# P V of both tiles in one matmul in two attention stages, and a normalisation moved to ScalarE

## The reference

```
x = x + tanh(g_xattn[i]) * attention_i(layernorm(x), ctx)
x = x + tanh(g_ffn[i])   * ffn_i(layernorm(x))
```

```
scores = q k^T / sqrt(8)          # 64 x 64; attention 2: where(mask, scores, -1e9)
attn   = softmax(scores)          # attention 3: stablemax
out    = attn v                   # 64 x 8
x      = x + gate * (cat(out over heads) Wo + bo)
```

## Time and profile before

| | us |
|---|---|
| median of 3 runs (2514.01 to 2516.51) | 2514.34 |
| profiled execution | 2513.01 |
| its span in the profile | 2511.2 |
| TensorE busy | 2146.8 (85%) |
| VectorE busy | 1787.9 (71%) |
| ScalarE busy | 1350.6 (54%) |
| GpSimd busy | 1157.7 (46%) |

### The profile page before, as it was taken

How to read it: one execution, slowest core, us unless ns; L and a number is a source line. 1 busy time by engine, 2 the same in 40 slices (tenths; PEclk the granted TensorE clock), 3 DMA queues, 4 the chain that set the end, 5 groups by cost and what they waited for, 6 DMA issues and landing times. The chain is left out here.

```text
span 2511.2 us, 81208 instructions
## 1 busy us (share of the span) xinstructions
PE 2146.8 (85%) x33432; PEld 1717.8 (68%) x33443; DVE 1787.9 (71%) x5105; ACT 1350.6 (54%) x2499; POOL 1157.7 (46%) x1712
## 2 busy tenths in 40 slices
PE   6999999999995969999555799998399958898597
PEld 5887878787874746777444577776399947777375
DVE  3777777777773648887896589886555559988354
ACT  3555555555551327886998455553122259979232
POOL 1333333434343541113776125555466666876444
PEclk8999999999997979998677899997699979989699
DMA  6330000000005621110000111111487622332363
GB/s 194 110 123 27 25 27 25 24 21 20 20 18 152 180 85 55 55 58 17 1 1 3 32 37 52 52 51 36 134 235 230 185 75 79 106 96 79 101 185 103
DMA packets 225233, 195.14 MB, mean 78 GB/s; under 512 B 34444, under 2 KB 197846, under 8 KB 224864
## 3 DMA queue, kind: packets, MB, share of 16 engines
q1 hardware_dynamic: 186336, 143.52, 19.6%
q0 software_dynamic: 18944, 36.98, 4.2%
q10 hardware_dynamic: 19584, 9.44, 1.3%
HBM read 113.53 MB, written 70.55 MB: 73 GB/s over the span
## 5 line engine op out<-in xcount | busy, mean ns | idle before, releaser
L617 POOL DMA_INDIRECT slots<-row,put x256 | 258.1, 1008 | 211.5 <-issue 131.2
L1968 PE MATMUL experts_H<-experts_xs_t,experts_w 128*128 128x256 f32 (+1 forms) x832 | 253.5, 456 | 9.9 <-DMA experts_w<-in_F_w 4.7
L1102 ACT ACTIVATE l_prob_t<-l_banks 128x512 f32<-128x512 f32 x256 | 132.2, 603 | 145.9 <-PE l_banks L1219 115.4
L1968 PEld LDWEIGHTS experts_H<-experts_xs_t,experts_w 128*128 128x128 f32 x832 | 156.7, 195 | 74.5 <-issue 54.0
L1474 POOL TENSOR_TENSOR l_var_eps<-l_mv,eps 128x1 f32<-128x1 f32 x64 | 12.1, 189 | 413.9 <-DVE l_mv L1555 413.9
L1277 PE MATMUL l_banks<-l_val,l_prob_t 128*64 128x18 f32 x5120 | 201.1, 215 | 0.0
L1277 PEld LDWEIGHTS l_banks<-l_val,l_prob_t 128*64 128x64 f32 x5120 | 190.3, 143 | 8.1 <-issue 0.7
L1510 DVE TENSOR_REDUCE l_top<-l_S 128x16 f32<-128x1024 f32 x64 | 78.3, 1224 | 161.7 <-PE l_S L1653 161.7
L1986 PE MATMUL experts_Y<-experts_w,experts_hid 128*128 128x128 f32 x1600 | 190.0, 275 | 3.5 <-DVE experts_y L1912 2.6
L1986 PEld LDWEIGHTS experts_Y<-experts_w,experts_hid 128*128 128x128 f32 x1600 | 184.3, 192 | 5.0 <-issue 4.9
L1823 POOL DMA_INDIRECT rows<-experts_y,experts_idx x144 | 139.9, 971 | 90.0 <-DVE experts_y L1908 52.9
(11 more groups left out here) (312 smaller groups left out, 5943.4 us busy)
## 6 DMA issues: line engine op xcount, KB each, us to landing
experts_w<-in_F_w SPq DMA_DIRECT2D x136, 256.0 KB
l_ctx_t<-in_ctx_t SPq DMA_DIRECT2D x96, 128.0 KB, 2.4
early_q_m<-l_q_t SPq DMA_DIRECT2D x384, 32.0 KB, 1.8
experts_xs<-slots SPq DMA_DIRECT2D x72, 132.0 KB
experts_w<-in_F_w ACTq DMA_DIRECT2D x72, 128.0 KB, 3.3
slots<-l_empty SPq DMA_DIRECT2D x16, 536.0 KB, 4.1
experts_xs<-slots SPq DMA_DIRECT2D x16, 536.0 KB
slots<-l_empty SPq DMA_DIRECT2D x16, 520.0 KB, 5.9
```

The lines of the kernel that those rows point to most:

```text
L617: pool.indirect_dma_start(self.slots, bass.IndirectOffsetOnAxis(ap=g.put[c][:, tile:tile + 1], axis=0), g.row[:, tile, self.sent_cols], No ...
L1102: nc.scalar.activation(prob_t[:, t.par(PROB), r, :], Z[:, r, :], ACT.Exp).then_inc(prob_done, 1)
L1968: last = nc.tensor.matmul(H[:, c, cols], w1_s[:, t.par(2, WS), h, c, :], xs_t[:, t.par(2), cols], start=True, stop=True)
```

## The change

- In the second and third attention (`not stable`), P V of a head is one matmul for both tiles: 128 columns of `prob_t` are stationary and 36 columns of `val` (both tiles) move. 16 matmuls take the place of 32. Of each result only the two diagonal blocks (tile 0's queries with tile 0's values, tile 1's with tile 1's) are used. The results lie in two banks (Z 2 and 3), 64 columns apart, so P V waits for the fourth exponential.
- The exponential writes its bank to `prob_t` in the order head, tile, query, so that the 128 columns of a head are next to each other.
- The reciprocal is over 64 columns instead of 32, and the scaling is two instructions of 64 partitions instead of one of 128.
- In the third attention the masks are one matmul of 512 columns for each bank, 4 for each set, instead of 8 of 256.
- In the third attention the two normalisations leave VectorE. GpSimd computes -mean * rstd in two small instructions for each, and ScalarE applies scale and bias, two instructions for each, at the end of its step.
- Waits: GpSimd's root waits for the earlier normalisation (`xn_done`), VectorE's aggregation for the earlier `shift_done`.

```diff
+    def shift_rows(self, nc, pool, t, s):
+        if t.live(s):
+            wait(pool, self.rstd_done, t.done(s))
+            nc.gpsimd.tensor_tensor(self.shift[...], self.mv[..., 0], self.rstd[...], ALU.mult).then_inc(self.shift_part, 1)
+            wait(pool, self.shift_part, t.done(s))
+            nc.gpsimd.tensor_scalar(self.shift[...], self.shift[...], -1.0, None, ALU.mult).then_inc(self.shift_done, 1)
+    def normalise(self, nc, act, t, s):
+        if t.live(s):
+            wait(act, self.shift_done, t.done(s))
+            for tile in range(self.tiles):
+                last = nc.scalar.activation(xn[...], x[...], ACT.Identity, bias=shift[...], scale=rstd[...])
+            last.then_inc(self.xn_done, 1)
...
-                    V.reciprocal(recip[:, :, :], o[:, :, :, 8]).then_inc(recip_done, 1)
+                    pairs = Z[:, 2:4, :].rearrange("p k (h c) -> p (k h) c", c=64)
+                    sums = o[:, :, :, 8] if stable else pairs[:, :, 8:36:9]
+                    V.reciprocal(..., sums).then_inc(recip_done, 1)
...
+                        for tile in range(2):
+                            rows = slice(64 * tile, 64 * tile + 64)
+                            pair = pairs[rows, :, 18 * tile:18 * tile + 18]...
+                            last = V.tensor_tensor(ctx_out[rows, ...], pair[:, :, :, 0:8], by..., ALU.mult)
+                        last.then_inc(o_drained, 1)
...
-                            nc.scalar.activation(prob_t[:, t.par(PROB), r, :], Z[:, r, :], ACT.Exp).then_inc(prob_done, 1)
+                            nc.scalar.activation(prob_t[:, t.par(PROB), r, :].rearrange("p (j t n) -> p t j n", t=2, n=64),
+                                                 Z[:, r, :].rearrange("p (t j n) -> p t j n", t=2, n=64), ACT.Exp).then_inc(prob_done, 1)
...
-                    for tile in range(2):
-                        for r in range(4):
-                            last = nc.tensor.matmul(Z[:, r, 256 * tile:256 * tile + 256], identity,
-                                                    hide[:, 1, 2 * t.item(PROB) + tile, :].unsqueeze(1).broadcast_to([P, 4, 64]), ...)
+                    masks = hide[:, 1, 2 * t.item(PROB):2 * t.item(PROB) + 2, :]
+                    for r in range(4):
+                        last = nc.tensor.matmul(Z[:, r, :], identity, masks.unsqueeze(2).broadcast_to([P, 2, 4, 64]),
+                                                start=False, stop=True)
...
-                        bank_read(t, 2)
+                        bank_read(t, 3)
+                    for h in range(16 if not stable else 0):
+                        pair = prob_t[:, t.par(OUT), h // 4, P * (h % 4):P * (h % 4) + P]
+                        last = nc.tensor.matmul(Z[:, 2 + h // 8, 64 * (h % 8):64 * (h % 8) + 36], pair,
+                                                val[:, t.par(OUT), :, h, :, :].rearrange("p t b c -> p t (b c)"), start=True, stop=True)
```

More of the change, by code:

```diff
@@ L563, in __init__ @@
         self.slots_clear = None
+        self.by_scalar = kind == "top2"
+        if self.by_scalar:
+            self.shift = ph.sb("tail_shift", [P, 2, tiles])
+            self.shift_part, self.shift_done = ph.sems("tail_shift_part tail_shift_done")
         self.loads = 16 * (1 + (bias is not None))
@@ L628, in root @@
             wait(pool, self.eps, t.done(s))
+            if self.by_scalar:
+                wait(pool, self.xn_done, t.done(s + 2))
             nc.gpsimd.tensor_tensor(self.rstd[:, t.par(s), :], self.var_eps[:, t.par(s), :], self.g.neg_half[:, 0:self.tiles],
                                     ALU.pow).then_inc(self.rstd_done, 1)
+    def shift_rows(self, nc, pool, t, s):
+        if t.live(s):
+            wait(pool, self.rstd_done, t.done(s))
+            nc.gpsimd.tensor_tensor(self.shift[:, t.par(s), :], self.mv[:, t.par(s), :, 0], self.rstd[:, t.par(s), :], ALU.mult).then_inc(
+                self.shift_part, 1)
+            wait(pool, self.shift_part, t.done(s))
+            nc.gpsimd.tensor_scalar(self.shift[:, t.par(s), :], self.shift[:, t.par(s), :], -1.0, None, ALU.mult).then_inc(self.shift_done, 1)
+    def normalise(self, nc, act, t, s):
+        if t.live(s):
+            wait(act, self.shift_done, t.done(s))
+            for tile in range(self.tiles):
+                last = nc.scalar.activation(self.g.xn[:, t.item(s) * self.tiles + tile, :], self.g.x[:, t.item(s) * self.tiles + tile, :], ACT.Identity,
+                                            bias=self.shift[:, t.par(s), tile:tile + 1], scale=self.rstd[:, t.par(s), tile:tile + 1])
+            last.then_inc(self.xn_done, 1)
     def finish(self, pool, items):
@@ L752, in dve @@
             wait(dve, self.part, n0)
+            if self.by_scalar:
+                wait(dve, self.shift_done, t.done(s + 2))
             for tile in range(k):
@@ L755, in dve @@
             last.then_inc(self.stats, 1)
-        if t.live(s + 1):
+        if t.live(s + 1) and not self.by_scalar:
             wait(dve, self.rstd_done, n1)
@@ L804, in attention_split @@
         var_eps, rstd = ph.sb("var_eps", [P, 2, 2]), ph.sb("rstd", [P, 2, 2])
+        shift = ph.sb("shift", [P, 2, 2]) if folded else None
+        shift_part, shift_done = ph.sems("shift_part shift_done") if folded else (None, None)
         xn, xn_t = ph.sb("xn", [P, 2, 2, D]), ph.sb("xn_t", [P, 2, 256])
@@ L920, in step @@
                     wait(pool, eps_done, t.done(NORM))
+                    if folded:
+                        wait(pool, xn_done, t.done(NORM + 2))
                     nc.gpsimd.tensor_tensor(rstd[:, t.par(NORM), :], var_eps[:, t.par(NORM), :], g.neg_half[:, 0:2],
@@ L924, in step @@
                     tail.root(nc, pool, t, T0 + 1)
+                if folded and t.live(NORM):
+                    wait(pool, rstd_done, t.done(NORM))
+                    nc.gpsimd.tensor_tensor(shift[:, t.par(NORM), :], mv[:, t.par(NORM), :, 0], rstd[:, t.par(NORM), :], ALU.mult).then_inc(shift_part, 1)
+                    wait(pool, shift_part, t.done(NORM))
+                    nc.gpsimd.tensor_scalar(shift[:, t.par(NORM), :], shift[:, t.par(NORM), :], -1.0, None, ALU.mult).then_inc(shift_done, 1)
+                if folded:
+                    tail.shift_rows(nc, pool, t, T0 + 1)
                 if head and t.live(1):
@@ L980, in statistics @@
                     wait(dve, stats_part, t.done(STAT))
+                    if folded:
+                        wait(dve, shift_done, t.done(STAT + 2))
                     for tile in range(2):
@@ L1062, in step @@
                                     ALU.add).then_inc(joined, 1)
-                if t.live(NORM) and not stable:
+                if t.live(NORM) and not stable and not folded:
                     normalise(t)
@@ L1141, in step @@
                     last.then_inc(turned_drained, 1)
+                if folded and t.live(NORM):
+                    wait(act, shift_done, t.done(NORM))
+                    wait(act, xv_filled, beats(t.t - 1, TURN, XV_BEATS))
+                    for tile in range(2):
+                        last = nc.scalar.activation(xn[:, t.par(NORM), tile, :], g.x[:, t.item(NORM) * 2 + tile, :], ACT.Identity,
+                                                    bias=shift[:, t.par(NORM), tile:tile + 1], scale=rstd[:, t.par(NORM), tile:tile + 1])
+                    last.then_inc(xn_done, 1)
+                if folded:
+                    tail.normalise(nc, act, t, T0 + 1)
             for t in range(FOLLOW + follower.STEPS if follower else STEPS):
@@ L1216, in step @@
                 if folded and t.live(PROB):
-                    for tile in range(2):
-                        for r in range(4):
-                            last = nc.tensor.matmul(Z[:, r, 256 * tile:256 * tile + 256], g.const_bf[:, C_IDENT:C_IDENT + P],
-                                                    hide[:, 1, 2 * t.item(PROB) + tile, :].unsqueeze(1).broadcast_to([P, 4, 64]),
-                                                    start=False, stop=tile == 1)
+                    masks = hide[:, 1, 2 * t.item(PROB):2 * t.item(PROB) + 2, :]
+                    for r in range(4):
+                        last = nc.tensor.matmul(Z[:, r, :], g.const_bf[:, C_IDENT:C_IDENT + P], masks.unsqueeze(2).broadcast_to([P, 2, 4, 64]),
+                                                start=False, stop=True)
                     last.then_inc(p_filled, 1)
                 if folded and t.live(SCORE):
[L1224 to L1228, removed]
+                    masks = hide[:, 0, 2 * t.item(SCORE):2 * t.item(SCORE) + 2, :]
+                    for r in range(4):
+                        last = nc.tensor.matmul(X[:, r, :], g.const_bf[:, C_IDENT:C_IDENT + P], masks.unsqueeze(2).broadcast_to([P, 2, 4, 64]),
+                                                start=False, stop=True)
                     last.then_inc(s_filled, 1)
@@ L1270, in step @@
                     else:
-                        bank_read(t, 2)
```

(6 more changed lines are left out.)

11 lines of the change are left out of this document (9 added, 2 removed).

## The result

The changed kernel takes 2748.2 us (median of 3 runs, 2744.34 to 2761.44) against 2514.3: a ratio of 1.094, 95% interval 1.0882 to 1.0998. It is slower, as forecast, but by 234 us where the forecast had 173, and outside the range, which ended at 2722.

What follows compares the result with a forecast made beforehand. TensorE's order of work was taken as the bound. Second attention 63, third 45 and edges 3 gave 2513.0 + 111 = 2624 us; the clock's 62 made it 2686, with a range for 8 of 10 of 2608 to 2722.

Steps and rivals of the forecast that it cites:

- reciprocal and scaling, second attention: On VectorE after P V: wider reciprocal +0.03, second scaling 0.34, less 0.05 us slack, so +0.35 us a step.
- whole without the clock: Whole kernel with the clock as it is: 2513.0 + 111 = 2624 us; the clock holding had chance 0.20.
- The bound: Second and third attention are bound by TensorE's order of work, with a few waits for VectorE in it.
- the sign: Whole kernel: slower 0.93, faster 0.05, within 5 us 0.02.
- P V's load: In P V, each load of 128 float32 columns takes 0.111 us, making P V 3.67 us, +1.62 per item.
- Masks: Third attention: halving the mask matmuls saves between 0 and 0.1 us a step; taken as 0.
- permuted store: The exponential's store in the new order: hidden, or 0.2 us a step in the second attention; taken as nothing.
- the normalisation's cover: Third attention: ScalarE's at most 1.9 us and GpSimd's 0.9 us a step, plus waits, are hidden.
- the +3 forecast for the ends: At the two ends of the third attention the normalisation's chain is bare: +3 us.
- VectorE's relief: Third attention: VectorE loses up to 1.4 us of normalisation a step, but gains nothing because TensorE's order sets the step.
- the clock's term: Second and third attention: clock falls in three steps of four, 1.3 us each: 64 x 0.75 x 1.3 = 62 us.
- long low stretches: Rival, chance 0.08: a quarter of the steps at 1.2 GHz, 112 us on top of 2624, 2736 or more.

Runs made afterwards that it cites:

- run 1: The changed kernel with 64 moving columns in each P V matmul instead of 36: 2646.8 us.
- run 4: The changed kernel with probabilities and values of P V in bfloat16 in the second and third attention, less precise: 2531.8 us.
- run 3: The changed kernel with P V, exponential, reciprocal and scaling as before, leaving only normalisation on ScalarE and masks of 512 columns: 2512.6 us.
- run 2: The kernel before with only the changed P V, permuted exponential, reciprocal and two scalings; masks and normalisation as before: 2746.6 us.
- run 6: The changed kernel with the transposes and values placed between heads 0 to 7 and heads 8 to 15 of P V: 2704.4 us.
- run 7: The kernel before with 9 moving columns in P V instead of 18 in the second and third attention: 2544.6 us.
- run 8: The kernel before with 32 moving columns in each P V matmul instead of 18 in all three attentions: 2496.0 us.
- run 5: The kernel before with the reciprocal over 64 values and the scaling in two instructions in the second and third attention: 2560.4 us.

## Why the prediction missed, step by step

| term | forecast | measured |
|---|---|---|
| P V, 128 float32 columns loaded 32 times | 3.67 us, +1.62 a step | 3.66 us |
| reciprocal and scaling, second attention | +0.35 a step | 1.52 - 0.95 = +0.57 |
| step of the second attention at full clock | 7.44 + 1.97 = 9.41 | 9.56 (run 1) |
| steps of the third at full clock | 11.87 and 12.03 | 11.96 and 12.13 (run 1) |
| whole without the clock | 2624 | 2646.8 (run 1) |
| what the clock takes, whole | 62 | 101 (2748.2 - 2646.8) |
| of it in the second attention | 31 | 36 |
| of it in the third | 31 | 65 |

The last two rows are read from the first and the last matmul of P V of a stage, of which the third attention's are shown (before, run 1, changed kernel):

```profile
L1277 PE MATMUL l_banks<-l_val,l_prob_t x2048: 210/211/291, 1421.9 to 1744.3; 128*64 128x18 f32 x187
L1334 PE MATMUL l_banks<-l_val_raw,l_prob_t x1024: 222/275/422, 1493.3 to 1863.5; 128*128 128x64 f32 x171
L1332 PE MATMUL l_banks<-l_val,l_prob_t x1024: 198/279/409, 1536.8 to 1972.0; 128*128 128x36 f32 x171
```

These are 322.4, 370.2 and 435.2 us; in the second attention they are 231.3, 304.7 and 340.7.

**Right.** The bound, the sign, and P V's load to 0.01 us; run 4 shows that it is the float32 load. Masks, permuted store and the normalisation's cover are right: run 3 is no different from before, run 2 loses as much as the whole change, and the one bare wait for the normalisation, 4.9 us at the beginning of the stage, stands near the +3 forecast for the ends. That VectorE's relief gives nothing is right for the whole time, not for a counting step (0.36 us, run 3). That the clock falls is right, and shown by runs 1, 6 and 7.

**Wrong: how long the clock stays low after a fall.** The step that failed is the clock's term, 64 x 0.75 x 1.3 = 62: "such a fall in three steps of four", each of 3.4 us as in the earlier trace rows. It took 101. The share was a choice and came out about right: from 1000 to 1130 us eight falls begin in 12 steps, from 1560 to 1860 us 19 in 21 steps. The length was wrong. In the third attention only one of the 19 lasts 3.4 us, 15 last 6.8 and three 10.2; in the second, five of the eight last 6.8. From the clock column the time at 1.2 GHz is (1 - 0.81) x 2 x 130 = 49 us, 4.1 a step, in the second and (1 - 0.77) x 2 x 300 = 138 us, 6.6 a step, in the third, where the forecast had 0.75 x 3.4 = 2.6. So the case worked out as a rival of low chance, long low stretches, came true in part.

The price of 1.3 us for 3.4 us of low clock was somewhat too high: third attention (14.3 - 12.05) / 6.6 = 0.34 us for each low microsecond, 1.2 for 3.4; in the second attention's steps from 1130 us on, with one fall of 3.4 us each, only some 0.7. That the second attention lost 36 us where 31 were forecast is therefore partly luck: longer falls at first, cheaper ones later.

I took the length of the falls among the steady steps for all. The trace before has a longer one in the third attention's last steps, and it was not priced:

```profile
1725.30:1732.10 6.80, 6.80 (x100) 4.64 (x98) 3.69 (x18) 0.37 (x1) 5.59 (x7) 0.50 0.16 51
```

Why a fall lasts longer behind the new P V than behind the old one stays open; run 1 shows that more moving columns in it end the falls, run 6 that another order shortens the time at the low clock.

**Wrong in size: the reciprocal, and the ends of the stages.** The reciprocal, priced at +0.03 for 32 more columns, is +0.20 (0.36 to 0.56 us), and the second scaling is 0.44 rather than 0.34. Run 1's profiled execution took 2640.0 us, 16 more than the 2624 that were worked out for a profiled execution; the other 7 of the 23 are the distance to the median of its four runs (2640.0 to 2649.6). Of the 16, the 0.15 us by which a step of the second attention is longer than forecast makes 5. Some 6 lie in its last four steps, 41.7 us in run 1 for 27.4 before, where four steps of +1.97 would give 7.9; two falls of 10.2 us stand there. The third attention adds 3 (47.8 for 45) and what lies outside of both stages 3 (6 for 3). A reading was off too: in the earlier trace rows L1051 starts 0.58 us after L1287's end, not 0.54, which is worth under 1 us in the sum; in run 1 it starts 0.30 to 0.34 after it, where 0.13 was forecast.

**The range** held the sum without the clock and ended 36 us above the forecast. Two terms of the same sign were under-priced together, the clock by 39 us and the rest by 23; the rival of long low stretches at 2736 or more had 0.08 and lay outside.

## What to carry to other kernels

Fewer matmuls are not faster if each loads more float32 columns: here two half-width loads go side by side in 58 ns a pass, a full-width one takes 111 to 118. Look for the spacing of weight loads in the trace before merging matmuls. Where loads set the spacing, more moving columns were free (64 for 36 in run 1, 32 for 18 in run 8), and they can pay by keeping TensorE's clock: 18 us here for one changed slice. When a change makes TensorE's stream thinner, price the clock as its own term, and look in the whole trace for the longest falls, not only for those among the steady steps.

## What was not expected of the hardware

- A reciprocal of 64 values a row took 0.56 us and one of 32 took 0.36: 6 ns for a value, where the scaling has 0.42 for 256.
- Two scalings on 64 partitions each, disjoint halves, took 0.86 us in a row, twice one on 128 partitions: they do not overlap.
- VectorE's 0.64 us a step cost 46 us in run 5. At full clock its steps account for about 36 of them: 32 x 0.59 in the second attention, 16 x 0.18 in the plain and 16 x 0.88 in the counting steps of the third. The rest goes with TensorE's lower clock, 0.95 and 0.96.
